# Vision-transformer layer on one core: front rearranged, router partly on ScalarE, other PSUM banks, expert and down products interleaved earlier

## The reference, cut to what matters

```
h = patches(x) @ W + b                                   # 16 images, 36 tokens each, D = 192
q, k, v = split(h @ w_qkv.T)                             # 12 heads of 64
q = q * rsqrt(norm(q over heads) + 1e-8); k likewise     # norm over axis 1, the heads
out = softmax(q k^T / scale[head]) v                     # within one image
h = layernorm(h + out @ w_out.T + b_out)
logits = h @ Wr + br; top 2 of 8 experts; softmax of the 2 logits
gate, up = h @ Wgu + bgu (clipped at 7); act = (up + 1) * gate * sigmoid(1.702 gate)
h = layernorm(h + sum over the 2 experts of weight * (act @ Wd + bd))
```

## Time and profile before

| | us |
|---|---|
| median of 3 runs | 186.21 |
| profiled execution, its own time | 187.39 |
| its span, first to last instruction | 185.7 |
| PE busy | 161.9 (87%) |
| DVE busy | 131.5 (71%) |
| ACT busy | 85.4 (46%) |
| POOL busy | 90.2 (49%) |
| mean granted clock of PE | 0.947 of 2.4 GHz |

### The profile page before, as it was taken

How to read it: one execution, slowest core, us unless ns; L and a number is a source line. 1 busy time by engine, 2 the same in 40 slices (tenths; PEclk the granted TensorE clock), 3 DMA queues, 4 the chain that set the end, 5 groups by cost and what they waited for, 6 DMA issues and landing times.

```text
span 185.7 us, 3415 instructions
## 1 busy us (share of the span) xinstructions
PE 161.9 (87%) x1252; PEld 142.8 (77%) x1252; DVE 131.5 (71%) x290; ACT 85.4 (46%) x156; POOL 90.2 (49%) x96
## 2 busy tenths in 40 slices
PE   7799998988985999689989899979879999999940
PEld 2498897977764897668769687859779999999930
DVE  0387799779496558998978588888965276376743
ACT  3367964645933446246444531724306244444610
POOL 7600592897354885375768484233316233144301
PEclk9999999999996699999965969999999999999997
DMA  6999975004200202011000000000000000000101
GB/s 175 321 312 253 282 208 175 0 0 97 78 0 2 88 2 88 0 33 52 4 0 0 5 0 0 4 0 0 0 4 0 0 4 4 0 0 4 48 0 48
DMA packets 4400, 10.62 MB, mean 57 GB/s; under 512 B 608, under 2 KB 1312, under 8 KB 4384
## 3 DMA queue, kind: packets, MB, share of 16 engines
q1 hardware_dynamic: 4384, 10.41, 19.5%
HBM read 9.96 MB, written 0.44 MB: 56 GB/s over the span
## 4 chain that ended last, share of the span: by engine, by line
PE 44%; DVE 30%; issue 9%; ACT 5%; DMA 5%; SPq 3%; POOL 1%; POOLq 0%; DVEq 0%; ACTq 0%
DVE sel L794 5%; DMA stage<-w_qkv_b 5%; PE ps L1139 4%; DVE reg_q L680 4%; PE ps L976 4%; PE ps L980 3%; PE ps L977 3%; PE ps L978 3%; PE ps L979 3%; PE ps L1080 3%; PE ps L1122 3%; DVE reg_p L662 3%; PE ps L1104 2%; DVE mx_r L722 2%; DVE reg_x L689 2%
## 5 line engine op out<-in xcount | busy, mean ns | idle before, releaser
L352 POOL TENSOR_TENSOR reg_r<-reg_q,reg_r 128x288 fp32r<-128x288 f32 x22 | 17.8, 813 | 30.0 <-ACT reg_r L536 30.0
L301 POOL TENSOR_TENSOR reg_w<-stage,reg_w 128x768 fp32r<-128x768 f32 x12 | 23.5, 1972 | 12.5 <-ACT reg_w L403 12.5
L817 DVE TENSOR_SCALAR reg_q<-ps,bup 128x288 f32<-128x288 f32 x24 | 12.3, 514 | 15.9 <-PE ps L980 15.9
L536 ACT ACTIVATE reg_r<-reg_q 128x288 fp32r<-128x288 f32 x24 | 10.6, 444 | 24.9 <-DVE reg_q L832 19.9
L330 POOL TENSOR_TENSOR reg_p<-reg_p,rinv 108x648 f32<-108x648 f32 (+1 forms) x12 | 14.8, 1233 | 14.7 <-DVE rinv L734 14.7
L1139 PE MATMUL ps<-wout,oT 128*108 128x192 f32 (+1 forms) x72 | 15.5, 373 | 1.7 <-DVE lg L773 1.4
L1139 PEld LDWEIGHTS ps<-wout,oT 128*108 128x108 f32 (+1 forms) x72 | 13.0, 193 | 3.0 <-issue 1.8
L976 PE MATMUL ps<-reg_r,reg_w 128*128 128x288 f32 x48 | 14.9, 310 | 0.1
L528 ACT ACTIVATE reg_q<-ps,sm 128x288 f32<-128x288 f32 x24 | 11.9, 496 | 6.0 <-PE ps L980 5.3
L722 DVE TENSOR_REDUCE mx_r<-ps 108x6 fp32r<-108x648 f32 (+1 forms) x12 | 9.1, 755 | 7.5 <-PE ps L1080 7.5
L403 ACT ACTIVATE reg_w<-stage 128x768 fp32r<-128x768 f32 x14 | 11.8, 845 | 5.2 <-DMA stage<-w_gu_a 1.9
(11 more groups left out here) (194 smaller groups left out, 492.5 us busy)
## 6 DMA issues: line engine op xcount, KB each, us to landing
reg_x<-xw_in SPq DMA_DIRECT2D x6, 416.0 KB, 6.6
stage<-w_gu_a SPq DMA_DIRECT2D x4, 384.0 KB, 5.0
stage<-w_gu_b SPq DMA_DIRECT2D x8, 192.0 KB, 3.7
stage<-w_qkv_a SPq DMA_DIRECT2D x3, 384.0 KB, 10.5
stage<-w_qkv_b SPq DMA_DIRECT2D x6, 192.0 KB, 9.9
stage<-w_down SPq DMA_DIRECT2D x3, 384.0 KB, 3.6
wout<-w_out SPq DMA_DIRECT2D x1, 576.0 KB, 13.1
out<-reg_q SPq DMA_DIRECT2D x6, 72.0 KB, 1.7
```

Source lines behind the costliest of these rows:

```text
L301: nc.gpsimd.tensor_tensor(dst[:, 1, :], raw, f(dst[:, 0, :]), ALU.subtract).then_inc(s_wlop, 1)
L352: nc.gpsimd.tensor_tensor(acts[:, n % NACT, 1], act_f[:, n % 4], f(acts[:, n % NACT, 0]), ALU.subtract).then_inc(s_alo, 1)
```

## The change

Front: GpSimd adds the k squares 7 to 9 only, VectorE adds 10 and 11 (`add_square_k`) behind its copies. ScalarE takes a root of one column (`warm`) ahead of `root(0)`, which now stands before `square(10)`. V copies 0 and 1 go to ScalarE; VectorE keeps 2, 3 and 5. `q_norm(1)` stands before the loop; the others move from even steps behind `sum_recip` to odd steps before it.

Router: it begins one step later. At even k from 6, behind `sum_recip(k)`, stand `read_logits` and `rank`; at odd k from 7 `router_weights`, now three small instructions. `sel` and its lines are gone; ScalarE's new `choose(g)` forms two one-hot rows, one for each chosen expert (Abs, Relu), five small activations, so that w2 has 16 rows. `onehot` and the bias rows are doubled for it.

Banks: h transpose, logits and the spread weights lie in bank 6 or 7, accumulators in 4 and 5, expert units in 0 to 3. `expert` on TensorE is split in `gate_up` and `spread`, on VectorE in `up_in`, `weigh`, `expert_act`. `down(0)` follows unit 4's `gate_up`, and then one down product follows nearly each unit.

```diff
-            for m in range(7, 12):
+            for m in range(7, 10):
                 add_square(m)
...
+            nc.scalar.activation(warm[:, :], sm[:, C_SCALE:C_SCALE + 1], ACT.Sqrt)
             act.wait_ge(s_const, 1)
+            root(0)
             square(10)
-            root(0)
             square(11)
             first_root(0)
+            v_evac(0)
             root(1)
+            v_evac(1)
...
+            def choose(g):
+
+                n = SIZES[g]
+                iota = sm[0:n, C_IOTA:C_IOTA + 8]
+                act.wait_ge(s_idx, g + 1)
+                if g >= 1:
+                    act.wait_ge(s_w2, 2 * g)
+                for j in range(2):
+                    nc.scalar.activation(far[0:n, j, :], iota, ACT.Abs, bias=rt[0:n, j:j + 1], scale=-1.0)\
+                        .then_inc(s_far, 1)
+                act.wait_ge(s_p1, g + 1)
+                nc.scalar.activation(p2[0:n, :], rt[0:n, 4:6], ACT.Copy, scale=rt[0:n, 3:4]).then_inc(s_p2, 1)
+                act.wait_ge(s_far, 2 * g + 2)
+                act.wait_ge(s_p2, g + 1)
+                if g >= 1:
+                    act.wait_ge(s_wt, g)
+                for j, prob in enumerate((rt[0:n, 4:6], p2[0:n, :])):
+                    nc.scalar.activation(w2[0:n, 0:64].rearrange("p (a e) -> p a e", a=2)[:, :, 8 * j:8 * j + 8],
+                                         far[0:n, j:j + 1, :].to_broadcast([n, 2, 8]), ACT.Relu,
+                                         bias=prob[:, 0:1], scale=prob[:, 1:2]).then_inc(s_w2, 1)
...
+            def add_square_k(m):
+
+                dve.wait_ge(s_ssk, m - 7)
+                nc.vector.tensor_tensor(ss[:, 1], ss[:, 1], sq[:, m % 3], ALU.add).then_inc(s_ssk, 1)
...
-                nc.vector.tensor_tensor(rt[0:n, 2:3], top[0:n, 1:2], top[0:n, 0:1], ALU.subtract).then_inc(s_gap, 1)
+                nc.vector.tensor_scalar(rt[0:n, 2:3], top[0:n, 1:2], top[0:n, 0:1], None, ALU.subtract)\
+                    .then_inc(s_gap, 1)
...
+            q_norm(1)
             for k in range(0, NU):
-                if k >= 4 and k % 2 == 0 and k // 2 - 2 < NG:
+                if k >= 4 and k % 2 == 0:
                     ln1_stats(k // 2 - 2)
...
+                if k in (1, 3, 5, 7):
+                    q_norm(k // 2 + 2)
+                sum_recip(k)
...
+                if k >= 6 and k % 2 == 0:
+                    read_logits(k // 2 - 3)
+                    rank(k // 2 - 3)
+                if k >= 7 and k % 2 == 1:
+                    router_weights(k // 2 - 3)
+                if k >= 5 and k % 2 == 1:
                     h1_lo(k // 2 - 2)
...
             p_transpose(11)
+            gate_up(0)
+            logits(3)
+            gate_up(1)
+            weighted(11)
             h1_transpose(4)
+            gate_up(2)
+            w_transpose(2)
+            project(5)
+            spread(0)
+            gate_up(3)
+            spread(1)
+            residual(0)
+            spread(2)
+            h1_transpose(5)
+            gate_up(4)
+            spread(3)
+            down(0)
```

More of the change, by code:

```diff
@@ L591, in _ @@
             expert(6)
-            w2_hi(5)
             act_hi(5)
-            for n in range(7, 2 * NT):
-                expert(n)
-                act_hi(n - 1)
+            w2_hi(3)
+            choose(4)
+            expert(7)
+            act_hi(6)
+            expert(8)
+            act_hi(7)
+            w2_hi(4)
+            choose(5)
+            for n in range(9, 2 * NT):
+                expert(n)
+                if n == NT + 4:
+                    act_hi(n - 1)
+                act_hi(n if n >= NT + 4 else n - 1)
+                if n == 10:
+                    w2_hi(5)
+                if n == NT + 2:
+                    z_copy(0)
                 if n == NT + 3:
-                    z_copy(0)
-                if n == NT + 4:
                     z_evac()
@@ L905, in _ @@
[L905 to L920 removed]
+            up_in(0)
+            read_logits(3)
+            rank(3)
@@ new lines, in _ @@
+            up_in(1)
+            router_weights(3)
+            h1_lo(4)
+            up_in(2)
+            w2_lo(2)
+            ln1_stats(5)
+            weigh(0)
+            expert_act(0)
+            ln1(5)
+            up_in(3)
+            weigh(1)
+            expert_act(1)
+            weigh(2)
+            expert_act(2)
+            h1_lo(5)
+            up_in(4)
+            weigh(3)
+            expert_act(3)
+            read_logits(4)
+            rank(4)
+            up_in(5)
+            weigh(4)
@@ new lines, in _ @@
+            expert_act(4)
+            router_weights(4)
+            read_logits(5)
+            up_in(6)
+            weigh(5)
+            expert_act(5)
+            w2_lo(3)
+            rank(5)
+            up_in(7)
+            weigh(6)
+            expert_act(6)
+            router_weights(5)
+            up_in(8)
+            weigh(7)
+            expert_act(7)
+            w2_lo(4)
+            for n in range(9, 2 * NT):
+                if n == NT + 4:
+                    weigh(n - 1)
+                    expert_act(n - 1)
+                if n < NT + 4:
+                    up_in(n)
+                    weigh(n - 1)
+                    expert_act(n - 1)
+                else:
+                    expert_in(n)
+                if n == 10:
@@ L1301, in _ @@
+            spread(4)
+            down(1)
+            logits(5)
+            gate_up(6)
+            spread(5)
+            down(2)
+            w_transpose(3)
+            gate_up(7)
+            spread(6)
+            down(3)
+            gate_up(8)
+            spread(7)
+            down(4)
+            w_transpose(4)
+            gate_up(9)
+            spread(8)
+            down(5)
+            down(6)
+            for n in range(10, 2 * NT):
                 if n == NT + 4:
                     residual(1)
+                    spread(n - 1)
@@ L1303, in _ @@
                     z_tiles(0)
-                if n < NT:
-                    for j in range(3 * n - 27, 3 * n - 24):
-                        down(j)
-                elif n > NT:
+                gate_up(n)
+                spread(n - 1 if n < NT + 4 else n)
+                if n == 10:
+                    w_transpose(5)
+                if n < NT + 3:
+                    down(n - 3)
+                elif n > NT + 3:
                     down(n - 4)
```

292 lines of the change are left out of this document (136 added, 156 removed).

## The result

The changed kernel takes **180.06 us** (median of 4 runs, 177.95 to 180.4), beside 186.31 for the kernel before on the same chip: ratio 0.963, 95% interval 0.954 to 0.972. Forecast was 177.7 in a range of 171.5 to 184. The profiled execution took 180.37 us with a span of 178.6.

The account below looks back on a forecast made before the run. It took VectorE router instructions held by GpSimd's queue to bound the loop, and matmuls from 136 to 175. Terms -6.5 - 1.6 + 1.7 + 0.9 - 2.5 - 0.5 = -8.5 us from 186.21 gave 177.7 us, range 171.5 to 184.

Parts of the forecast that it names:

- held until GpSimd's queue was empty: Main theory: some VectorE instructions on SBUF wait until GpSimd's queue is empty, whatever their size; forecast 177.7 us, 50%.
- rival A: GpSimd gives way after each instruction, so casts wait 0.5 us at most, q_norms under 1; 172.5 us, chance 17%.
- Loop, -6.5 and +1.7 of low clock: Attention loop, inverse of unit 3 to 11: 35.5 us for 42.0, less 1.7 lost to one stretch at 1.2 GHz.
- 35 to 37: Sign set for the new profile: us from the inverse of unit 3 to that of unit 11.
- rival B: Router in the loop: the cast takes L794's place, held until GpSimd's queue is empty; 182.4 us, chance 23%.
- Half clock of `project(4)`, -1.6: Second low-clock stretch, at 108.1: idle before it goes with L794's 4.08 us, so 3.16 us of half-speed work gains 1.6.
- Front, +0.9: Before unit 3: PE waits up to 2.5 us for `norm_sum(1)` and may drop to 1.2 GHz; 0.9 us slower.
- Up to unit 3 these cancel: Front: additions 2 us late, against V copies moved to ScalarE and no PE idle of 2.12 us before unit 2.
- Expert stage, -2.5: Down products fill PE holes before 136, 3.3 us in all, less perhaps 0.8 for a shared spread bank: 2.5 us faster.
- my 4.6: Forecast gain from inverse 11 to the end of the span: -1.6 - 2.5 - 0.5 = -4.6 us.
- PE idle under 1 us in all: Sign set for the new profile: PE idle between the first and twelfth expert unit, with clock 1.00 there.
- The end, -0.5: Last `act_hi` waits 0.89 us for VectorE's product behind `act_lo(22)`; the product now comes first: 0.5 us faster.

Follow-up runs that it names:

- measurements behind the end: Three runs of the changed kernel with added rounds timing one VectorE instruction beside queued GpSimd work; cast 1.67 us beside subtractions, 4.29 behind `probs`; total time means nothing.
- third measurement: Changed kernel plus 21 rounds after its end, taking `probs` apart: cast held 4.29 us with large subtractions behind `probs`, 0.77 with three of 128x192.
- late down products: Changed kernel with down products back in their old places, none before unit 9, then three behind each of units 9 to 11: 182.5 us, ratio 0.9759.
- four fixes: Changed kernel with all k additions on GpSimd, index cast on ScalarE, root(4) and w2(2) work earlier, three z_scale behind last act_hi: 175.6 us, ratio 0.9400.

## Why the prediction was right where it was, and wrong where not

**Which theory.** I had "held until GpSimd's queue was empty" as the forecast and "gives way after each instruction" as rival A. The measurements behind the end show both: A for plain instructions, the forecast for what comes into `probs` with large instructions right behind it. All the long holds of the loop, before and after, came into `probs` (72.30 to 73.03, 88.53 to 88.71 and 108.74 to 108.92 before; 89.88 to 90.48 and 71.37 to 72.13 after), but not all that came into it were held for long. Timeline before: L794 in step 6, 0.18 us into `probs` (78.49), and what GpSimd does behind it.

```profile
78.67 1.17 DVE L794 SCALAR_TENSOR_TENSOR sel<-sm,rt,sel 108x8 f32<-108x8 f32 x1
79.73 1.26 POOL L293 TENSOR_TENSOR reg_r<-stage,reg_r 128x512 fp32r<-128x512 f32 x1
```

It got through at the end of `probs`, as it did at 99.34, again 1.17 us ahead of a 128x512. So did the cast of step 6 after (0.70 us, ahead of a `k_norm` of 128x216). Behind the `probs` of the long holds stood a 128x768 or a 128x648 (in step 8 with the power between them). The third measurement agrees at its two sizes (768 held, 192 not); what decides in between was not tried. The two additions in the front are A's case too: 1.67 us, then 2.28 more, one `w_lo` each. The Trainium skill (SBUF — State Buffer, section "SBUF: two separate sides") has the lock held for a whole instruction; the 1.67 us beside one, two and four subtractions agree, and the 4.29 us behind `probs` do not.

**Loop, -6.5 and +1.7 of low clock: right, -4.5 measured against -4.8** (37.5 us, just outside the 35 to 37 that I had set as a sign). By groups: 9.97, 8.62, 10.68, 8.21 us against my 9.1, 9.8, 9.0, 7.6. Two terms were too small. `q_norm(4)` I took at 1.75; it was 2.72. I had it come "when `probs` is over", and it came 0.76 us into `probs`. The cast of step 8 I took at 1.2 and it was 2.98, my own upper bound of 2.9 and the sign I had set for rival B (over 2.5). B as a whole did not come: the casts of steps 6 and 10 took 0.70 and 0.17, not 1.9 and 2.1, all three together 3.85 us against my 3.2 and B's 6.9. The group 5 to 7 gave 1.2 us back: 0.3 by the cast and 0.4 by the small `q_norm` (0.37 for my 0.8); the rest I can't assign. The one low stretch is there, 94.5 to 97.9, behind the held cast; what it costs by itself no run separates. That errors of both signs left -4.5 so near -4.8 is luck.

**Half clock of `project(4)`, -1.6: right.** At 103.37 it takes 2.20 us where it took 3.68.

**Front, +0.9: failed, -0.8.** What I said of `norm_sum(1)` held: 42.80 for my 43, with 1.2 GHz behind it from 43.3. The step that failed is "Up to unit 3 these cancel". I had read the low clock from 66.5 on only. Before, PE stood at 1.2 GHz also from 56.9 to 63.7; the fall came in its 2.12 us of idle, while a held `q_norm` stood ahead of row_max(2). A stretch of it, and that `q_norm` on VectorE, both before:

```profile
57.00:63.50 6.50, 5.57 (x36) 4.61 (x37) 4.26 (x8) 1.39 (x3) 3.92 (x3) 0.50 0.04 9
54.59 2.55 DVE L680 TENSOR_TENSOR reg_q<-reg_q,rnorm 128x648 f32<-128x648 f32 x1
```

After, row_max(2) stands ahead of its `q_norm`, PE has no such idle, and that stretch is gone. Where the low stretch at 43 did not come, inverse 3 stands at 63.9 to 64.1, 2.4 us before where it was. How much of this the V copies on ScalarE gave, no run separates.

**Expert stage, -2.5: the size was right, the sum was not.** The late down products cost 3.1 us by the medians. But in their profile only 1.7 us of the tail are holes, against my 2.5; the rest came by PE's clock, which my sum for this stage did not have. So the size is in part luck. And the tail as a whole gave 1.7 of my 4.6. I let the stage begin with all its inputs ready; "what is late next" I had not asked. GpSimd's `root(4)` stood behind a `w_lo(15)` and a `w_lo(16)` of 1.8 and 2.0 us, `ln1(4)` waited 2.16, and `project(5)` 1.01 for the second w2. Moving both gave 1.1 us back. The signs I set, PE idle under 1 us in all, missed: it is 2.3 us, in the four waits at 110.93 (0.35), 114.20, 119.60 (0.26) and 131.96, at clock 1.00.

**The end, -0.5: failed, -0.1.** From the last `up` to the last `act_hi` it was 2.34 us before (173.75 to 176.09) and is 2.22. The product no longer stands behind `act_lo(22)`, but behind the last gelu, which stands behind three `z_scale` of 1.41 us together: the product waits 0.65 us, and `act_hi` behind it still 0.53 where it had waited 0.89. Moving them behind it gave 0.56 us back, in the run of the four fixes.

**What holds the sum together.** -8.5 forecast, -7.1 in the span. The front was 1.7 better and the tail 2.9 worse than I said, so that the total came so close is luck in part. The main step is shown by its undoing: selection on VectorE, 186.5 us.

## What to carry to other kernels

Move an instruction off the engine that another one can hold, and ask of the one that remains in its chain what it meets: the cast stayed on VectorE, took L794's place in one step of three, and cost 2 us until it went to ScalarE too. A hold is priced by when the instruction comes: look which GpSimd instruction runs at that moment, and what is ready behind it. A gain in the middle of a kernel arrives only if the next stage's first inputs come earlier as well; list them, with the queue that each stands in.
